# Eight token-count sizes in place of six in a routed feed-forward kernel

## The reference

```python
xr = rotate(x)                                 # [2048, 256]
top1 = argmax(softmax(xr @ router_w + router_b))
for i in range(8):
    h = xr @ w1[i] + b1[i]                     # w1[i] is 256 x 2048
    a, g = split(h, 2)
    y = (a * sigmoid(g)) @ w2[i] + b2[i]       # w2[i] is 1024 x 256
    out += where(top1 == i, y, 0)
return x + out
```

## Time and profile before

| what | value |
|---|---|
| runs | 214.12, 214.83, 215.44 us |
| profiled execution | span 213.9 us from first to last instruction; no other time of it is given |
| TensorE busy | 202.7 us, 95% |
| VectorE, ScalarE, GpSimd busy | 158.0, 122.5, 129.2 us (74, 57, 60%) |
| the first product's first matmul | 36.3 us into the span |
| instruction queue q8 | 7 packets, 0.11 MB |

### The profile page before, as it was taken

One profiled execution on the slowest core, in us unless ns is written; L12 is line 12 of the kernel. 1 busy time (PEld: TensorE's weight loads), 2 busy tenths in 40 slices (PEclk: granted clock), 3 DMA queues, 4 the chain that ended last, 5 costly groups with the idle time before them and its releaser, 6 DMA issues.

```text
span 213.9 us, 4367 instructions
## 1 busy us (share of the span) xinstructions
PE 202.7 (95%) x1512; PEld 191.0 (89%) x1513; DVE 158.0 (74%) x308; ACT 122.5 (57%) x206; POOL 129.2 (60%) x163
## 2 busy tenths in 40 slices
PE   7997779999999999999998999999999999999991
PEld 3877625999999999999998999899999999999991
DVE  4918936789928996598888969993998479874950
ACT  2454861576727482667585767564949185735620
POOL 6002467876802888287878877885487817820751
PEclk9999969999999999999999999999999999999998
DMA  5993744889775174937499479738535691820011
GB/s 144 393 365 122 291 142 116 265 300 311 215 193 227 63 259 97 361 90 264 103 296 317 131 219 320 259 76 292 223 135 168 204 287 69 256 44 0 25 40 37
DMA packets 17540, 41.26 MB, mean 193 GB/s; under 512 B 2920, under 2 KB 11241, under 8 KB 15338
## 3 DMA queue, kind: packets, MB, share of 16 engines
q1 hardware_dynamic: 12784, 30.48, 39.9%
q0 software_dynamic: 4512, 10.50, 19.4%
q10 hardware_dynamic: 218, 0.01, 0.1%
HBM read 36.78 MB, written 6.03 MB: 200 GB/s over the span
## 4 chain that ended last, share of the span: by engine, by line
PE 57%; POOL 13%; DVE 12%; issue 7%; DMA 7%; ACT 2%; DVEq 0%; POOLq 0%; ACTq 0%
PE y_ps L1121 7%; DMA xg<-x_rows,g_idx 7%; PE y_ps L1122 6%; PE y_ps L1123 6%; POOL y_out L429 5%; PE g_ps L1101 5%; POOL out_dram L438 5%; PE g_ps L1106 5%; PE g_ps L1102 4%; PE a_ps L1106 4%; PE a_ps L1102 4%; PE a_ps L1101 4%; PE y_ps L931 3%; POOL xg L417 3%; DVE arena L821 3%
## 5 line engine op out<-in xcount | busy, mean ns | idle before, releaser
L438 POOL DMA_INDIRECT out_dram<-y_out,s_idx x30 | 42.1, 1403 | 41.5 <-DVE y_out L850 30.8
L573 ACT ACTIVATE arena<-g_ps,b_t 128x384 f32<-128x384 f32 (+1 forms) x64 | 34.5, 538 | 47.4 <-PE g_ps L1106 47.4
L821 DVE SCALAR_TENSOR_TENSOR arena<-a_ps,b_t,arena 128x384 f32<-128x384 f32 (+1 forms) x64 | 36.1, 564 | 30.5 <-PE a_ps L1106 27.6
L1121 PE MATMUL y_ps<-w_hi,u_hi 128*128 128x256 f32 x168 | 48.6, 289 | 0.1
L429 POOL DMA_INDIRECT y_out<-in_x_dram,g_idx x32 | 42.4, 1325 | 9.8 <-issue 9.8
L1122 PE MATMUL y_ps<-w_lo,u_hi 128*128 128x256 f32 x168 | 47.5, 283 | 0.0
L1123 PE MATMUL y_ps<-w_hi,u_lo 128*128 128x256 f32 x168 | 47.5, 283 | 0.0
L417 POOL DMA_INDIRECT xg<-x_rows,g_idx x32 | 37.2, 1164 | 13.7 <-issue 9.1
L712 DVE TENSOR_TENSOR w_lo<-w_raw,w_hi 128x1024 fp32r<-128x1024 f32 x32 | 37.2, 1220 | 4.8 <-DMA xg<-x_rows,g_idx 3.6
L579 ACT ACTIVATE u_hi<-arena 128x384 fp32r<-128x384 f32 (+1 forms) x64 | 30.7, 479 | 15.5 <-DVE arena L821 15.5
L1101 PE MATMUL g_ps<-xr_hi,w_hi 128*128 128x256 f32 (+3 forms) x128 | 36.9, 301 | 0.3 <-issue 0.2
(11 more groups left out here) (167 smaller groups left out, 297.0 us busy)
## 6 DMA issues: line engine op xcount, KB each, us to landing
w_raw<-in_L_ffn_w_dram SPq DMA_DIRECT2D x16, 1024.0 KB, 8.5
w_raw<-in_L_ffn_w_dram SPq DMA_DIRECT2D x16, 512.0 KB, 5.0
arena<-in_x_dram SPq DMA_DIRECT2D x4, 512.0 KB, 5.9
x_rows<-arena SPq DMA_DIRECT2D x8, 256.0 KB, 2.6
b_all<-in_L_ffn_b_dram SPq DMA_DIRECT2D x1, 1024.0 KB, 5.1
xg<-x_rows,g_idx POOLq DMA_INDIRECT x32, 6.1
y_out<-in_x_dram,g_idx POOLq DMA_INDIRECT x32, 4.2
out_dram<-y_out,s_idx POOLq DMA_INDIRECT x30, 4.0
```

The costliest lines, as they stand in the source:

```text
L438: nc.gpsimd.indirect_dma_start(out=out_flat, out_offset=bass.IndirectOffsetOnAxis(ap=s_idx[:, i * NSUB + s:i * NSUB + s + 1], axis=0), in_ ...
L573: nc.scalar.activation(sig[:, c % SIG_RING, 0:n], pair[c % RING][1][:, 0:n], ACT.Sigmoid, bias=b1_t[:, bass.ds(e * (2 * NC) + (NC + c), 1) ...
L821: V.scalar_tensor_tensor(u32[:, c % (8 - SIG_RING), 0:n], pair[c % RING][0][:, 0:n], b1_t[:, bass.ds(e * (2 * NC) + c, 1)], sig[:, c % SIG ...
L1121: T.matmul(dst, u_hi[:, uv], w2_hi[:, wv], start=first, stop=False)
```

## The change

The list of sizes goes from six to eight, every leaf gets a landing, and three more visits stand in the prelude.

```diff
-    SIZES = (256, 288, 320, 352, 384, 512)
+    SIZES = (224, 256, 272, 288, 304, 320, 336, 512)
...
-    LANDINGS = (0, 1, 2, 3, 5)
+    LANDINGS = tuple(range(len(SIZES)))
...
                 if f == 3:
                     visit(2)
+                if f == 6:
+                    visit(7)
...
                 rotate_blocks(b)
+                if b == 3:
+                    visit(8)
                 if b == 5:
                     visit(4)
+                if b == 6:
+                    visit(9)
```

## The result

| | before | after |
|---|---|---|
| median of the runs beside each other, us | 214.80 (4 runs, 214.12 to 215.44) | 289.06 (4 runs, 288.29 to 290.49) |
| ratio | | 1.344, 95% interval 1.337 to 1.352 |
| span of the profiled execution, us | 213.9 | 288.7 |
| TensorE busy, idle, us | 202.7, 11.2 | 218.1, 70.6 |
| mean granted clock of TensorE | 0.987 | 0.867 |

The change is 34% slower. Of the 74.8 us by which the span grew, TensorE's idle time is 59.4 and its busy time 15.4. In time: the prelude is 23.4 us longer, pass 1 by 23.1, pass 2 by 10.2, pass 3 by 2.6, pass 6 by 3.4, pass 7 by 10.8, pass 8 by 2.0, while passes 4 and 5 are shorter by 0.4 and 0.1 (each pass from its first matmul to the next one's).

A forecast was written before the change was run, and what follows sets the result against it. Bounds: TensorE's columns in some passes, VectorE in 5, 6 and 8, GpSimd's transfers at pass 4's end. Gains -2.4, visit 7 +1.6, other code +0.2: -0.6 us, 214.83 to 214.2, no change; range 211.0 to 219.5.

The forecast's parts named there:

- The columns: First products of passes 2 to 8: fewer columns save 2.4 us on the path, between 1.8 and 2.7.
- the floor taken from the rotation: First-product matmuls at 224 columns: 111.5 ns each, after the prelude rotation's 111 ns, not the slope's 106.7.
- passes 2 to 4: Gain of 0.95 us in sum; the other 1.3 us become a longer wait for the gather, GpSimd being late.
- The wait for the gather at the end of pass 4: TensorE's wait before the transposes for pass 5, expected to grow from 0.6 to about 2 us.
- Passes 5 and 6: VectorE starts chunk 2 earlier and its line stays as long: 0.24 us gained each, 0.4 becomes waiting.
- the return to the loop's head: Branch back at each pass's end, seven returns: no cost counted; over 0.4 us a return would fail the forecast.
- the case where it is hidden: Second product's last block, 24 matmuls, 2.9 us, queued whole, covers a 2.6 us code wait at each return.
- visit 7: Prelude, ahead of the eighth transposes and router product: TensorE waits for absent code, 1.6 us, between 0 and 3.6.
- visits 8 and 4: Other visits in the prelude: cost nothing if the code parts they enter are there.
- the read-ahead: TensorE's sequencer runs ahead of the array by at least 0.48 us, perhaps 1.5, hiding some of the wait at visit 7.
- The code no longer stays: Rival, chance 0.21: the longer loop pushes out its own code, so returns wait; 221 us at 1.0 us a return.
- The rival of 289 us: Rival, chance 0.06: float32r under 256 columns runs at float32's pace, 377 ns a matmul, 74 us more.

The follow-up runs named there:

- e1: Kernel before with six sizes as before at other values (224, 256, 272, 320, 336, 512), program and five visits kept: 212.81 us, ratio 0.992.
- e13: The change's eight sizes, four unused leaves moved behind the loop, only the four near leaves with landings, visited in program order: 212.83 us, 0.991 of the kernel before.
- e12: e1 with 200 in place of 224 columns: 213.14 us, 0.992 of the kernel before.
- e4: Kernel before plus three small matmuls (six instructions) in TensorE's prelude, moving landing 2 from 705 to 711: 225.9 to 235.0 us, ratio 1.053.
- e7: The change with seven sizes (without 288), visits 7 and 8 kept, 2,122 instructions: 276.56 us, 1.291 of the kernel before.
- e10: Kernel before with 24 never-executed matmuls in the loop's last part, 1,969 instructions: 215.16 us, ratio 1.001.
- e11: Kernel before with 40 never-executed matmuls in the loop's last part, 2,001 instructions: 216.9 and 235.0 us in two runs.
- e9: e1 with 200 never-executed matmuls behind the loop, 2,322 instructions: 213.30 us, 0.991 of the kernel before.

## Why the prediction was wrong

**The columns: right.** Forecast were 2.4 us; e1 measured 1.8 (1.0 to 2.6), e13 2.0 (1.4 to 2.6). Steps of six matmuls take 0.67 us at 224 columns, 0.76 at 272 and 0.93 at 336, so the floor taken from the rotation held, and e12 shows it to be one. By passes, e1 against before: passes 2 to 4 together 1.07 us less (forecast 0.95), pass 7 0.63 (0.64), pass 8 0.43 (0.31).

**Passes 2 to 4.** The wait for the gather at the end of pass 4, 0.60 us in the earlier trace rows, was forecast to grow to about 2; it grew to 1.37:

```profile
113.32 0.33 PE L1057 MATMUL a_ps<-ident,xg 128*128 128x128 f32 x1 [1.37 <-DMA xg<-x_rows,g_idx]
...
132.88 0.32 PE L1057 MATMUL a_ps<-ident,xg 128*128 128x128 f32 x1 [0.47 <-DMA xg<-x_rows,g_idx]
```

**Passes 5 and 6: no gain.** Forecast were 0.24 us each, with VectorE as the limit; measured 0.05 less and 0.18 more. VectorE is the limit as forecast. The second row above is a wait in pass 5 that wasn't there before, but it costs nothing, because the second product, behind it, waits for VectorE's last low part, as in the earlier trace rows (chain of waits in e1):

```profile
135.80 0.57 DVE u_lo L827
...
136.41 0.39 PE y_ps L1121
```

In both passes VectorE starts chunk 2 0.16 us earlier after the pass's start, not 0.24, and takes as long as before or up to 0.05 more. What is left of the gain, and more in pass 6, goes between there and the next pass's first matmul; why is open.

**The steps that failed.** The forecast's sum put the return to the loop's head at nothing (it "holds the case where it is hidden") and counted one missed part in the prelude, at visit 7. Measured, the passes take 51.4 us more than before and the prelude 23.4.

**The visits.** The prediction gave visit 7 1.6 us, and "nothing, if the parts they enter are there" to visits 8 and 4.
- Visit 2 was not looked at, because it isn't new. Four instructions more ahead of it moved its landing from 705 to 709, over the edge of a part; e4 shows what such a step costs.
- The condition of the others was not worked out. Visits that jump ahead and back, to 7, 3, 8, 4, 9, wait at every one, 3.8 to 5.6 us in the branch.
- The price of one, forecast at 1.6 us, came out at 3.05 and 3.17 and within its range, by two errors that offset each other. The wait was put at 2.6 us and the read-ahead at 0.48 to 1.5. The branches of visits 2 and 7 take some 6 us:

```profile
L938 PEldq COMPARE_BRANCH  x2: 5649/5876/6102, 7.0 to 14.0; - x2
```

TensorE works on what is queued until 10.46 and 16.88, which hides 3.5 and 2.9 us of it, and the holes are left. In e7 a branch as long (6.05 us from 11.48) had only 0.8 us of work ahead of it, and nearly all of it is a hole:

```profile
18.15 1.10 PE L967 MATMUL g_ps<-ident,arena 128*128 128x128 f32 x4 [5.88 <-issue]
```

- The prediction said that the trace of before doesn't show such a wait. It did: the row of line 938 has a branch of 2.27 us, the visit at 29.6, beside a packet that starts at 29.5.

**The return to the loop's head: a rival with the right mechanism, mis-sized.** "The code no longer stays" had a chance of 0.21 and a price of 221 us, 232 at most, from 2.6 us at each of seven returns. The holes at the returns are 17.17, 9.45, 0, 0, 0, 3.45 and 5.93 us. A return to absent code misses one part after the other, the loop's head, the branch of the tree, the leaf. The branches in front of pass 2, which take at most 0.22 us in the kernel before:

```profile
L1158 PEldq COMPARE_BRANCH  x1: 8027/8027/8027, 87.2 to 87.2; - x1
...
L1168 PEldq COMPARE_BRANCH  x1: 2655/2655/2655, 95.8 to 95.8; - x1
...
L1153 PEldq COMPARE_BRANCH  x2: 2979/3554/4129, 99.1 to 103.3; - x2
```

TensorE has work until 89.4, so 2.2 us of the first are hidden; the other three have nothing queued ahead of them. Passes 4 to 6 use leaves that lie close together, and their code stays. On top come the visits and the lower clock behind each hole, which the rival left out.

By the Trainium skill (Runtime: NRT & Kernel Launch, section Instruction fetch mechanics) TensorE's instruction memory holds 2,048 instructions and is filled in blocks of 256; e10 and e11 agree with that size. It also says that a taken branch out of the current window of two blocks has to wait; there e10 disagrees, where seven returns from the program's eighth part to its second fetched nothing (no packet after the seventh). The prediction gave the rule as one for the whole program's length, and there e9 and e13 disagree: 2,322 and 2,315 instructions cost nothing when the loop's stretch is short.

**The rival of 289 us** (float32r under 256 columns) hit the number by luck: 224 columns cost 112 ns a matmul, not 377.

**Open.** The rule of eight parts gives 31 fetches for the change and 7 for e4; 43 and 13 were measured. After a visit to an absent part more is lost than first in, first out explains. In e11, where no visit takes more than 1.8 us, the same rule gave over 30, and 20 were measured. e4's and e11's times differ from run to run. So the number of parts that stay and the request for the next one fit the runs, but which part leaves wasn't settled.

## What to carry to other kernels

Where a program branches at run time, lay out the engine's code as carefully as its data: count the instructions from the loop's head to its end, keep that stretch with what is ahead of it within what the instruction memory holds (here 2,029 was free, and 2,061 cost some 20 us in one run of two), and put variants that are rarely taken behind the loop. Code fetched ahead by visits is best visited in the order of the program, with time between the visits, and a few instructions more in front can move a landing into a part that isn't there, so the positions are to be counted anew with every edit. In the profile, read the packets of the engine's instruction queue and the rows of its branches: a branch of microseconds, with a hole released by "issue" and a packet beside it, is absent code.

## What the runs showed of the hardware

- An absent part leaves TensorE idle for 1.8 to 4.4 us in the change where one is met by itself, and for 5.88 us in e7; the packet itself took 0.95 us of it behind visit 2.
- Work queued ahead of such a branch shortens the hole: branches of 6.10 and 5.65 us left 3.05 and 3.17 us idle in the change, one of 6.05 us with 0.8 us of work ahead left 5.88 in e7.
- Eight parts stay: 2,029 instructions are fetched once in e10 (7 packets), and with 2,061 code is fetched again in the profiled run of e11 (20).
- In and behind a hole the clock was granted at its lower level: 0.50 from 92.4 to 109.4 us, where TensorE was idle until 106.59. The matmuls of the change are 21.8 us longer busy than the same ones in e13.
- float32r matmuls of 200 and of 224 columns start every 111.5 and 111.6 ns; 256 took 120.
- Executions of one program that fetches code again can differ by 18 us (e11: 216.9 and 235.0).
